# Two attention layers with 512-column query products, one unsplit value product and the output projection four steps behind

## The reference

```python
q = (latents @ Wq).reshape(b, q_len, 4, 8, 128)          # 32 query heads of 128, 4 key/value heads
k, v = hidden @ Wk, hidden @ Wv                          # hidden = context and latents, 128 keys for each sequence
attn = softmax(einsum('bqhgd,bkhd->bhgqk', q, k) / sqrt(128))
out = einsum('bhgqk,bkhd->bqhgd', attn, v).reshape(b, q_len, 4096) @ Wo
```

## Time and profile before

| | us |
|---|---|
| median of 3 runs (lowest to highest) | 1805.06 (1804.2 to 1806.93) |
| the profiled execution's own time | 1810.68 |
| its span (first to last instruction) | 1808.9 |
| TensorE matmul busy | 1594.0 (88%) |
| TensorE weight load busy | 1330.0 (74%) |
| VectorE busy | 952.2 (53%) |
| ScalarE busy | 698.4 (39%) |
| GpSimd busy | 628.2 (35%) |
| mean granted TensorE clock | 0.948 |

### The profile page before, as it was taken

The page is one execution under the profiler, slowest core; times in us unless marked ns, Lnnn a source line. Parts: engine busy times, 40 slices in busy tenths (PEclk is TensorE's granted clock), DMA queues, the critical chain, the costliest instruction groups (busy, mean ns, idle before and its releaser), DMA issues. The chain is left out here.

```text
span 1808.9 us, 29350 instructions
## 1 busy us (share of the span) xinstructions
PE 1594.0 (88%) x10450; PEld 1330.0 (74%) x10450; DVE 952.2 (53%) x1857; ACT 698.4 (39%) x2015; POOL 628.2 (35%) x594
## 2 busy tenths in 40 slices
PE   5887879859699999999999996968999999999976
PEld 4655666548588988888888895757778877877853
DVE  4885668777424322331432326686565656655653
ACT  3443154344335435443452533442333234224221
POOL 2542244475313212321331321334343534434410
PEclk9997999969899999999999999879999999999986
DMA  5001110021301100110000001231112112211001
GB/s 193 1 1 47 40 37 1 1 85 52 85 27 48 36 24 25 44 39 19 30 24 24 25 24 54 98 88 59 59 35 74 54 35 81 70 54 39 13 3 47
DMA packets 27865, 81.14 MB, mean 45 GB/s; under 512 B 3248, under 2 KB 11952, under 8 KB 22768
## 3 DMA queue, kind: packets, MB, share of 16 engines
q1 hardware_dynamic: 26896, 79.44, 13.2%
q10 hardware_dynamic: 864, 0.30, 0.1%
HBM read 69.25 MB, written 10.49 MB: 44 GB/s over the span
## 5 line engine op out<-in xcount | busy, mean ns | idle before, releaser
L386 PE MATMUL bank<-hid_high,wq_high 128*128 128x256 f32 x1152 | 343.6, 298 | 6.5 <-DVE probs_last L1181 5.8
L386 PE MATMUL bank<-hid_low,wq_high 128*128 128x256 f32 x1152 | 327.1, 284 | 0.0
L386 PE MATMUL bank<-hid_high,wq_low 128*128 128x256 f32 x1152 | 327.0, 284 | 0.0
L386 PE MATMUL bank<-wo_high,out_high 128*128 128x512 f32 x576 | 241.5, 419 | 43.5 <-DVE out_low L1231 37.6
L1239 DVE SCALAR_TENSOR_TENSOR x_stream<-bank,gates,x_stream 128x512 f32<-128x512 f32 x128 | 96.1, 751 | 266.6 <-PE bank L386 266.6
L386 PEld LDWEIGHTS bank<-hid_high,wq_high 128*128 128x128 f32 x1152 | 221.9, 193 | 14.4 <-issue 10.1
L386 PE MATMUL bank<-wo_low,out_high 128*128 128x512 f32 x576 | 230.8, 401 | 0.0
L386 PE MATMUL bank<-wo_high,out_low 128*128 128x512 f32 x576 | 229.8, 399 | 0.0
L1025 POOL TENSOR_TENSOR probs_middle<-probs_middle,small 128x512 f32<-128x512 f32 x64 | 66.7, 1042 | 458.4 <-DVE small L1226 458.4
L386 PEld LDWEIGHTS bank<-hid_low,wq_high 128*128 128x128 f32 x1152 | 222.3, 193 | 2.9 <-issue 2.9
L386 PEld LDWEIGHTS bank<-hid_high,wq_low 128*128 128x128 f32 x1152 | 221.8, 193 | 0.0
(11 more groups left out here) (255 smaller groups left out, 3504.2 us busy)
## 6 DMA issues: line engine op xcount, KB each, us to landing
raw_q<-in_L_wq SPq DMA_DIRECT2D x18, 1024.0 KB, 5.1
raw_o<-in_L_wo SPq DMA_DIRECT2D x18, 1024.0 KB, 4.9
values_last<-ctx_values SPq DMA_DIRECT2D x32, 256.0 KB, 3.9
values_t_last<-ctx_keys SPq DMA_DIRECT2D x8, 512.0 KB, 5.3
raw_c<-in_L_wkv SPq DMA_DIRECT2D x6, 512.0 KB, 5.3
x_stream<-in_x SPq DMA_DIRECT2D x8, 256.0 KB, 9.8
ctx_keys<-raw_o SPq DMA_DIRECT2D x8, 256.0 KB, 2.0
ctx_values<-raw_o SPq DMA_DIRECT2D x16, 128.0 KB, 2.4
```

Of the source, the lines that this page charges most:

```text
L386: last = k.nc.tensor.matmul(out, stationary(a, c), moving(b, c), start=n == 0, stop=n == total - 1)
```

## The change

The query products take eight batches and one head at a time, 12 matmuls of 512 columns, and their results go to two buffers that hold four tiles each; scores of tile t wait for all four products of their half. The second buffer is `queries_t2` in the third layer, and in the fourth it is made of the free half of `values_t` and of `raw_c`; the load of the next stage's router weights into `raw_c` therefore waits for the last scores. Four query products are made ahead instead of three. In the third layer probabilities and values stay float32 and `attend` has one matmul for each of two halves. The output projection and the update run in step t+4 instead of t+3, and all units have 12 steps. The next query weights are split in steps 4 and 4 to 5, and VectorE rotates the next keys ahead of the update. Cut to its core (lines moved left, unchanged lines mostly left out):

```diff
@@ before line 161
-        self.pt = [sb("probs_t_high", 1024, F32R), sb("probs_t_low", 1024, F32R)]
-        self.vj = [sb("values_high", 2048, F32R), sb("values_low", 2048, F32R)]
+        self.pt, self.vj, self.q2 = sb("probs_t", 1024), sb("values", 2048), sb("queries_t2", 2048)
     else:
@@ before line 875
-Q = k.q[:].rearrange("p (a h n) -> p a h n", a=2, h=4)
-Q2 = k.q[:].rearrange("p (a g b h n) -> p a g b h n", a=2, g=2, b=4, h=2)
+if rope:
+    Q = [[k.q[:, D * i:D * i + D] for i in range(4)],
+         [k.vt[:, 1024 + D * i:1024 + D * i + D] for i in range(2)] + [k.raw_c[:, D * i:D * i + D] for i in range(2)]]
+else:
+    Q = [q[:].rearrange("p (g b h n) -> p g b h n", g=2, b=8, h=2) for q in (k.q, k.q2)]
@@ before line 888
 else:
-    PT = [t[:].rearrange("p (a n) -> p a n", a=2) for t in k.pt]
-    V = k.vj
+    PT = [k.pt[:].rearrange("p (a n) -> p a n", a=2)]
+    V = [k.vj]
@@ before line 898
+LAG_Y = LAG + 2
...
 if rope:
-    KV_AT, BACK_AT, Q_AT = {}, {}, {8: [0], 9: [1], 10: [2]}
+    KV_AT, BACK_AT, Q_AT = {}, {}, {7: [0], 8: [1], 9: [2], 10: [3]}
 else:
-    KV_AT, BACK_AT, Q_AT = {6: [0], 7: [1], 8: [2, 3], 9: [4, 5], 10: [6, 7]}, {10: [0, 1], 11: [2, 3]}, {11: [0, 1, 2]}
-SLOTS = T + LAG + (1 if rope else 2)
-AHEAD = 3
+    KV_AT, BACK_AT, Q_AT = {6: [0], 7: [1], 8: [2, 3], 9: [4, 5], 10: [6, 7]}, {10: [0, 1], 11: [2, 3]}, {11: [0, 1, 2, 3]}
+SLOTS = T + LAG_Y
+AHEAD = 4
...
 def part(table, t, i):
@@ before line 943
         if rope:
-            fetch_ahead(k, sp, NEXT[f"L{layer}"], "c")
@@ before line 954
+            fetch_ahead(k, sp, NEXT[f"L{layer}"], "c", k.s_psum, k.at("s_psum", 8 * kv_heads))
         else:
@@ before line 997
             else:
-                r = n - NT
-                if r >= 4:
-                    pool.wait_ge(k.s_psum, v("s_psum", j, 8 * UN, 2 * (r // 2) - 2))
-                out = Q[:, (r // 2) % 2, 2 * (r % 2):2 * (r % 2) + 2, :].rearrange("p h n -> p (h n)")
+                half, head = divmod(n - NT, 4)
+                pool.wait_ge(k.s_psum, v("s_psum", j, 8 * UN, 4 * half - 4))
+                out = Q[half][head]
@@ before line 1027
-                    if t in (5, 6) and not (last and u == UN - 1):
-                        low_q(j, u + 1, 2 * (t - 5), 2 * (t - 5) + 2)
+                    if t in (4, 5) and not (last and u == UN - 1):
+                        low_q(j, u + 1, 2 * (t - 4), 2 * (t - 4) + 2)
@@ before line 1072
         def value_back(j, n):
...
-            nc.scalar.copy(V[0][:, 512 * n:512 * n + 512], k.bank[2 + n % 2][:]).then_inc(k.v_hi, 1)
+            nc.scalar.copy(V[0][:, 512 * n:512 * n + 512], k.bank[2 + n % 2][:]).then_inc(k.v_sbuf, 1)
...
         def queries(j, u, q):
-            p, h = divmod(q, 2)
-            act.wait_ge(k.q_psum, v("q_psum", j, 8 * UN, 8 * u + 2 * p + h + 1))
-            nc.scalar.activation(Q2[:, p % 2, h].rearrange("p b h n -> p h b n"),
-                                 k.bank[4 + h][:].rearrange("p (h b n) -> p h b n", h=2, b=4), ACT.Copy,
+            half, head = divmod(q, 4)
+            act.wait_ge(k.q_psum, v("q_psum", j, 8 * UN, 8 * u + q + 1))
+            nc.scalar.activation(Q[half][:, head // 2, :, head % 2, :],
+                                 k.bank[4 + q % 2][:].rearrange("p (b n) -> p b n", b=8), ACT.Copy,
@@ before line 1115
-                    nc.scalar.copy(PT[0][:, t % 2], k.bank[2 + t % 2][:, 0:4 * KEYS]).then_inc(k.pt_sbuf if rope else k.pt_hi, 1)
+                    nc.scalar.copy(PT[0][:, t % 2], k.bank[2 + t % 2][:, 0:4 * KEYS]).then_inc(k.pt_sbuf, 1)
...
                 def out_high(t):
@@ before line 1124
                 ahead = u == UN - 1 and not last
-                for t in range(SLOTS if ahead else T + LAG + 1):
+                for t in range(SLOTS):
...
                     if t < T:
@@ before line 1137
-                    if t == 5 and not (last and u == UN - 1):
+                    if t == 4 and not (last and u == UN - 1):
@@ before line 1150
-                    if t >= T and not rope and u < UN - 1:
-                        queries(j, u + 1, t - T)
+                    if T - 1 <= t < T - 1 + AHEAD and not rope and u < UN - 1:
+                        queries(j, u + 1, t - T + 1)
@@ before line 1186
         if rope:
...
-        def value_low(j, n):
-            dve.wait_ge(k.v_hi, v("v_hi", j, NT, n + 1))
-            cols = slice(512 * n, 512 * n + 512)
-            nc.vector.tensor_tensor(V[1][:, cols], k.bank[2 + n % 2][:], V[0][:, cols],
-                                    ALU.subtract).then_inc(k.v_sbuf, 1)
-        if not rope:
-            for n in range(NT):
-                value_low(0, n)
...
         def queries(j, q):
             if rope:
@@ before line 1239
-                def probs_low(t):
-                    dve.wait_ge(k.pt_hi, v("pt_hi", j, 8 * UN, 8 * u + t + 1))
-                    nc.vector.tensor_tensor(PT[1][:, t % 2], k.bank[2 + t % 2][:], PT[0][:, t % 2],
-                                            ALU.subtract).then_inc(k.pt_sbuf, 1)
                 ahead = u == UN - 1 and not last
-                for t in range(SLOTS if ahead else T + LAG + 1):
+                for t in range(SLOTS):
                     if t < T:
...
-                    if not rope and LAG <= t < T + LAG:
-                        probs_low(t - LAG)
+                    if rope and 6 <= t < 6 + NT and not last:
+                        key(j + 1, t - 6)
...
-                        for n in () if rope else part(BACK_AT, t, 0):
-                            value_low(j + 1, n)
-                    if LAG + 1 <= t <= T + LAG:
-                        update(t - LAG - 1)
-                    tile = t - LAG - 2
+                    if LAG_Y <= t:
+                        update(t - LAG_Y)
+                    tile = t - LAG_Y - 1
...
-                    if rope and 6 <= t < 6 + NT and not last:
-                        key(j + 1, t - 6)
...
-                        for n in () if rope else part(BACK_AT, t, 1):
-                            value_low(j + 1, n)
@@ before line 1307
         def queries(j, u, q, first=False):
-            p, h = divmod(q, 2)
+            half, head = divmod(q, 4)
             if rope:
-                if p:
-                    pe.wait_ge(k.rope_mul, v("rope_mul", j, ROPES, NT + 2 * p + h - 1))
+                if q >= 2:
+                    pe.wait_ge(k.rope_mul, v("rope_mul", j, ROPES, NT + q - 1))
                 elif not first:
-                    pe.wait_ge(k.rope_mul, v("rope_mul", j, ROPES, h - 1))
+                    pe.wait_ge(k.rope_mul, v("rope_mul", j, ROPES, q - 1))
...
-            elif p or u:
-                pe.wait_ge(k.q_sbuf, v("q_sbuf", j, 8 * UN, 8 * u + 2 * p + h - 1))
+            elif q >= 2 or u:
+                pe.wait_ge(k.q_sbuf, v("q_sbuf", j, 8 * UN, 8 * u + q - 1))
             else:
-                pe.wait_ge(k.kv_sbuf, v("kv_sbuf", j, 2 * NT, 2 * NT - 1 + h))
+                pe.wait_ge(k.kv_sbuf, v("kv_sbuf", j, 2 * NT, 2 * NT - 1 + q))
...
-            for i in (2 * h, 2 * h + 1):
-                last_mm = product(k, k.bank[4 + h][:, 256 * (i % 2):256 * (i % 2) + 256],
-                                  lambda s, c: k.wq[s][:, c * D + i * P:c * D + (i + 1) * P],
-                                  lambda m, c: hid_cols(k, m, c, 4 * p, 4, 1), C)
-            last_mm.then_inc(k.q_psum, 1)
+            product(k, k.bank[4 + q % 2][:], lambda s, c: k.wq[s][:, c * D + head * P:c * D + (head + 1) * P],
+                    lambda m, c: hid_cols(k, m, c, 8 * half, 8, 1), C).then_inc(k.q_psum, 1)
...
         for t in range(T):
@@ before line 1339
         if rope:
...
+            queries(0, 0, 3)
         else:
@@ before line 1352
         def body(j, last):
...
                 def scores(t):
-                    p = t // 2
+                    half = t // 4
                     if rope:
-                        pe.wait_ge(k.q_sbuf, v("q_sbuf", j, ROPES, NT + 2 * p + 2))
+                        pe.wait_ge(k.q_sbuf, v("q_sbuf", j, ROPES, NT + 4 * half + 4))
                     else:
-                        pe.wait_ge(k.q_sbuf, v("q_sbuf", j, 8 * UN, 8 * u + 2 * p + 2))
+                        pe.wait_ge(k.q_sbuf, v("q_sbuf", j, 8 * UN, 8 * u + 4 * half + 4))
                     if rope:
...
-                                rows, tok = slice(S * c, S * c + S), P * (t % 2) + S * c
+                                rows, tok = slice(S * c, S * c + S), P * (t % 4) + S * c
...
-                                                           Q[:, p % 2, i, tok:tok + S],
+                                                           Q[half][i][:, tok:tok + S],
...
                     else:
@@ before line 1371
-                                                       Q2[:, p % 2, i % 2, b % 4, :, :],
+                                                       Q[half][:, i % 2, b % 8, :, :],
@@ before line 1399
                     else:
...
-                            for n, (s, m) in enumerate(PAIRS):
```

(16 more changed lines are left out.)

## The result

The changed kernel takes **1821.42 us** (median of four runs, 1814.82 to 1823.56), the one before 1805.69 beside it: 1.0081 times as long, 95% interval 1.0054 to 1.0109. Timed again with more runs it was 1817.03 (five runs, 1814.97 to 1818.86) against 1805.02, 1.0066 [1.0053, 1.0079]. So it is 12 to 16 us slower where I forecast no change: above my range (1793 to 1817) in the first measurement, at its upper edge in the second.

The account below looks back on a forecast made before the run. Both attention layers were taken to run at TensorE's pace. Terms gave +6.2 (third) and -3.0 (fourth), together +3.2, or -2.6 by whole units; the middle, 0, gave a forecast of 1805, eight in ten between 1793 and 1817.

Parts of the forecast that it names:

- the last one of the sum: Both layers: middle of +3.2 and -2.6 taken as 0, half-speed stretches as now, so 1805.
- the wait, 2.3 in step 3: Fourth layer: scores(4) wait for query 7 through VectorE's rotation and GpSimd's add, 2.3 x 8 = +18.
- the price of a stretch: Fourth layer: a half-speed stretch costs 1.4 and has followed waits of 2.1.
- rival A: New waits in step 3 pull the clock down in every unit and head: +15, 1820; chance 11%.
- not four to nine: Sign that the forecast is wrong: half-speed stretches of the two layers outside four to nine.
- Low query weights: Fourth layer: TensorE waits for the next head's split query weights in step 7, 0.65 x 7 = +4.6.
- no wait for the low output: Projection in step t+4 no longer waits for the low output: -36.5 in the fourth layer.
- the update, 0.94 for 0.95: A unit's last projection waits for the single output bank's update: 0.95 x 8 = +7.6 in the fourth layer.
- first scores of the layer: Fourth layer: four queries before the first scores start them +6.6 later, +3.7 net of the body's 2.9.
- the count by pieces: Whole units added piece by piece: -2.6 together; third-layer unit 65.6, head 63.2, both last ones 6 to 7 shorter.
- Width in all: Both layers: query products of 512 columns, 0.10 less each, -13 in all; bounds nothing and -20.

Follow-up runs that it names:

- lag_split: The kernel before with the output projection in step t+4 and the next query weights split one step earlier; 1789.38 us, 0.9914.
- lag_only: The kernel before with only the output projection and its update in step t+4 and 12 steps for each unit; 1829.18 us, 1.0122.
- Width alone: The changed kernel with each query product in two halves of 256 columns, buffers and waits unchanged; 1831.18 us, 1.0154.

## Why the prediction was wrong

**The step that failed** is the last one of the sum: "I take the middle, 0, and the half-speed stretches as they are now". I had the wait, 2.3 in step 3 of every head of the fourth layer (measured 2.24), and I had the price of a stretch, 1.4, and named as rival A that the two would meet. I gave it 11%. What the runs showed in its place: with the wait, all eight heads have a half-speed stretch behind scores(4) in both profiles of after; with the wait filled, none, and 14.2 us less. The argument against rival A, that the third layer's step 2 waits 1.40 at full clock, compares the wrong thing. It is an argument about the third layer, and there it was right: no unit of after has a stretch. In the fourth layer the wait is 2.24 with a 0.54 before it, and the nearest row was the earlier trace rows, behind a wait of 2.1 in the same layer. It should have had the larger part there. That the length of a wait alone does not decide it is shown by the kernel with five ahead: waits of 1.4 are followed by half speed in four of eight heads of the fourth layer. Rival A's own 1820 is near the result partly by accident: it counted 16 stretches and there are 8, and the low weights paid for the rest. Of the signs that I had set, "not four to nine" half-speed stretches is met by the second profile alone (ten; the first has nine).

**Point by point, fourth layer** (forecast 503 us from first scores to last update, which is 512.8 less 10; measured 516.5; 512.8 and 516.5 are means of two profiles each):

- The clock: the 14 us that the filled wait gave back, less the 7 of the kernel before that the forecast left standing: +7.
- Low query weights, mis-sized: 1.4 in seven waits where I had 0.65, 9.7 us instead of 4.6: +5. GpSimd's second pair of low parts begins 3.4 after scores(6), as I said, but it takes longer. This is the view of GpSimd and then of VectorE beside it:

```profile
1404.56 0.97 POOL L1027 TENSOR_TENSOR probs_last<-probs_last,small 128x256 f32<-128x256 f32 x1 [1.31 <-DVE small L1218]
1405.50 3.39 POOL L983 TENSOR_TENSOR wq_low<-raw_q,wq_high 128x512 fp32r<-128x512 f32 x2
```

```profile
1405.08 1.01 DVE L1182 TENSOR_TENSOR probs_last<-values_t_last,rope 64x512 f32<-64x512 f32 x1
1406.10 1.66 DVE L1183 TENSOR_TENSOR probs_last<-values_t_last,rope 64x512 f32<-64x512 f32 x1
1407.79 0.75 DVE L1231 SCALAR_TENSOR_TENSOR x_stream<-bank,gates,x_stream 128x512 f32<-128x512 f32 x1
```

  3.39 against 2.52 (that row is the first pair of before, in step 5, whose place the second takes here). In before VectorE waited for the projection at that time and rotated only afterwards; now the rotation of the keys runs beside the subtraction, and both are slower (the rotation's last product 1.66 instead of 0.68). 0.65 and 0.87 are 1.5, measured 1.4. Two other runs fit: in `lag_split`, where the rotation begins only behind the start of the second subtraction, the pair takes 2.5 (1.28 and 1.29), and in `lag_only`, where the rotation runs beside both, 3.4 (1.71 and 1.71), although it stands behind the update there. I had noted the move of the rotation and asked only whom it delays on its own engine.
- The rest, 1.3, I have not divided.
- What held: scores(4) 2.24 for 2.3; no wait for the low output; the update, 0.94 for 0.95; first scores of the layer 5.8 later for 6.6, means of two (the wait for query 3 is 3.6).

The Trainium skill (SBUF — State Buffer, "Who interferes with whom") says that a VectorE instruction with two inputs in SBUF contends with a GpSimd instruction that reads SBUF, and that the later one blocks until the first is done. The rows agree, with more in them than that: the two engines take turns. The rotation's two products end at 1406.1 and 1407.8, and each subtraction ends 1.1 behind one of them, at 1407.2 and 1408.9; the second product begins at 1406.1 and ends 0.5 to 0.6 behind the first subtraction. So each waited for the other's instruction before it.

**Third layer** (forecast +5.4 in the stage, measured -2.6): the pieces were right (value product 0.86, waits 0.75 and 0.77, unit 65.79 for 65.6). A unit followed by queries became 1.0 to 1.05 longer, as said, except one that in before has a half-speed stretch of 1.6 us in the first profile. The last unit is 6.2 shorter, as the count by pieces had it, for the 3.2 that its terms make. For the three units followed by key and value products I had +1.4 each. One of them has it (87.0 to 88.38). The other two did not grow (88.6 and 89.1 to 88.46 in the first profiles), because before has in front of the next unit's first scores a wait that after has not (view of the waits in the third layer of before):

```profile
PE pair L1373 <- issue: 3.4, 2, 2.0
```

The sum has no term for these two waits, 1.44 and 1.98: it puts them at nothing without a word. All the kernels with 256-column query products in this layer have them (3.3 to 4.1 us in two), the halved one of "Width alone" included, and none with 512 columns has. So they belong to the width; what TensorE waits for there no view shows. Width in all was 14.2 for 13.

**Where the gain went.** The order of the work (projection and split) is worth -16 alone, the width about -14, the unsplit product some +3. Their sum would be -27, and after measures +12: 39 us are between them. Stage by stage against the kernel with the new order alone, after is 27.5 us longer in the fourth layer (516.5 for 489.0), 7 between the layers, where query 3 is now made and waited for, and 3.5 up to the third; the third layer itself is 9.5 shorter (583.3 for 592.8). So the loss is in and just ahead of the fourth layer: 17.9 us of waits for query 7, nine or ten half-speed stretches and 9.7 of waits for the low weights, of which the new order alone has none. The wait for query 7 comes from the requirement of four ready queries. That the kernel with five ahead gives back 39 too is partly chance: about 15 of it is the tail, whose wait for the update the new order alone has as well (7.1 us in nine), and in return it keeps waits of 1.4, five stretches and the wait for the weights. What the requirement costs by itself no run isolates.

In the order of before two query products fill the buffer of two tiles, so scores(4) need query 5, made in step 2; in that of after four products fill a buffer of four tiles, so they need query 7, made in step 3. With five ahead query 7 is made in step 2 again.

**What stays open.** The third layer's new form measured +0.26% once and +0.04% once, with the same stage; its two profiled executions differ in how many half-speed stretches the fourth layer had, which none of the edits explains. Nor do the runs say why the same wait is followed by half speed in one head and not in another (1.4 us with five ahead, 2.24 with the halves of 256). The change also moved the router weights' load and the keys' rotation; neither was tried alone.

## What to carry to other kernels

A wait on TensorE has two prices, its own length and what the clock does behind it, and the second can be found by putting idle matmuls in its place: if the time falls while the awaited instruction starts no earlier, it was the clock. When a buffer is made wider, count how many of its producers the first consumer needs, and move the production ahead by as much; here one query earlier was worth 39 us, nearly three times the gain of the width itself, though only some half of it lay at that consumer. After such a move, count every step again: the unit's tail gained as well, because a product came between two projections that shared one bank. And before a step is moved, look for what runs on the neighbour engine at its new time, not only for what is queued behind it.

## What the runs showed of the hardware that I had not expected

- The granted clock falls to 0.50 behind a wait of 2.24 us (0.54 before it, TensorE busy 1.20 of 3.40) in eight of eight heads of both profiles of after, in seven of eight of the kernel with halves of 256 columns and the same wait, and in four and six of eight behind a wait of 1.4 (five ahead, and with the earlier split). It stays at 1.00 in the third layer behind two waits of 0.75 and 0.77 with 1.1 of work between them. Matmuls that nobody reads, in the wait, keep it at 1.00 in eight of eight.
- A pair of subtractions on GpSimd takes 3.39 instead of 2.52 us when VectorE does products of two tiles beside it, and these take up to 1.66 instead of 0.68: each waits for the other engine's instruction to end.
- Two float32 products of 128x128 by 256 columns, four records, take 0.86 us start to start, 0.43 each, where three reduced-precision matmuls in place of each took 0.35.
- Two waits of 1.4 to 2.0 us in front of a unit's first scores, which the profile puts to nothing, come and go with the width of the query products: 3.3 to 4.1 us in six kernels with 256 columns in the third layer, none in those with 512.
